# A graph layer whose lists are loaded in two parts, with its edges and pieces of x in another order

## The reference

```python
msg = node_feat[src] + edge_feat                       # 53125 x 128
neigh = segment_sum(msg, dst, num_segments=3125)
rst = (1.0 + eps[0]) * node_feat + neigh
h = rst @ W1 + b1                                      # 256 columns
h = (h - mean(h, 0)) * rsqrt(var(h, 0) + 1e-5) * gamma + beta
out = relu(h) @ W2 + b2
x = layernorm(x + out, axis=-1)
```

## Time and profile before

| | us |
|---|---|
| median of three runs (256.85 to 257.66) | 257.31 |
| the profiled execution, its own time | 256.49 |
| its span, first to last instruction | 254.6 |
| PE busy | 238.1 |
| DVE busy | 184.7 |
| POOL busy | 172.5 |
| ACT busy | 130.1 |

### The profile page before, as it was taken

The page is one execution under the profiler, slowest core; times in us unless marked ns, Lnnn a source line. Parts: engine busy times, 40 slices in busy tenths (PEclk is TensorE's granted clock), DMA queues, the critical chain, the costliest instruction groups (busy, mean ns, idle before and its releaser), DMA issues.

```text
span 254.6 us, 6682 instructions
## 1 busy us (share of the span) xinstructions
PE 238.1 (94%) x2080; PEld 197.2 (77%) x2080; DVE 184.7 (73%) x706; ACT 130.1 (51%) x229; POOL 172.5 (68%) x114
## 2 busy tenths in 40 slices
PE   7579999899999999999999999999999999999980
PEld 3569678788889988888878888888888888644970
DVE  2899888998989888887878777865757311388872
ACT  2343366665556655655544544544443320386794
POOL 4667557888888888888888888888888870550000
PEclk9755699999999999999999999999999999999998
DMA  4799878988988988887878887878676320000033
GB/s 114 237 243 238 223 175 196 260 218 180 213 190 184 209 183 209 192 193 189 198 168 178 190 190 165 188 164 179 155 162 130 63 36 8 0 0 5 0 126 130
DMA packets 38189, 40.00 MB, mean 157 GB/s; under 512 B 5330, under 2 KB 25864, under 8 KB 38152
## 3 DMA queue, kind: packets, MB, share of 16 engines
q1 hardware_dynamic: 23176, 32.70, 44.3%
q0 software_dynamic: 14400, 6.56, 21.5%
q10 hardware_dynamic: 576, 0.28, 0.5%
HBM read 37.92 MB, written 1.60 MB: 155 GB/s over the span
## 4 chain that ended last, share of the span: by engine, by line
PE 66%; DVE 8%; POOL 7%; DMA 7%; issue 5%; ACT 3%; DVEq 1%; SPq 1%; ACTq 0%; POOLq 0%
PE ps L736 21%; PE ps L745 17%; PE ps L772 9%; POOL egat L538 7%; PE ps L766 6%; PE ps L715 4%; PE ps L844 4%; DMA ebuf<-in_edge_lists_dram 3%; DVE hit_k L1043 2%; PE ps L830 2%; PE ps L763 2%; DMA egat<-in_x_dram,srci 2%; DVE aggT L1125 2%; DMA aggT<-in_x_columns_dram 2%; PE ps L696 2%
## 5 line engine op out<-in xcount | busy, mean ns | idle before, releaser
L538 POOL DMA_INDIRECT egat<-in_x_dram,srci x100 | 162.9, 1629 | 42.6 <-issue 27.1
L624 ACT ACTIVATE big<-ps 128x500 f32 x158 | 96.4, 610 | 91.0 <-PE ps L772 89.8
L745 PEld LDWEIGHTS ps<-hit_c,ebuf 128*128 128x128 f32 x632 | 104.5, 197 | 13.9 <-DVE aggT L1125 4.5
L745 PE MATMUL ps<-hit_c,ebuf 128*128 128x12 f32 (+1 forms) x632 | 96.9, 228 | 5.3 <-DMA ebuf<-in_edge_lists_dram 2.7
L1125 DVE TENSOR_TENSOR aggT<-aggT,ps 128x20 f32 x208 | 36.1, 173 | 47.3 <-PE ps L745 35.3
L736 PE MATMUL ps<-big,xN 128*128 128x120 f16 (+7 forms) x200 | 58.2, 293 | 0.3 <-ACT big L624 0.3
L736 PE MATMUL ps<-big,xr 128*128 128x120 f16 (+7 forms) x200 | 58.3, 293 | 0.0
L736 PE MATMUL ps<-big,x_room 128*128 128x120 f16 (+7 forms) x200 | 58.2, 293 | 0.0
L772 PE MATMUL ps<-hit_k,hit_l 128*128 128x375 f16 x158 | 55.3, 350 | 0.0
L766 PE MATMUL ps<-hit_k,hit_l 128*128 128x300 f16 x158 | 47.0, 297 | 0.0
L1043 DVE TENSOR_TENSOR hit_k<-iota_b,key 128x752 f16<-128x752 f16 x79 | 43.1, 546 | 0.2
(11 more groups left out here) (95 smaller groups left out, 182.3 us busy)
## 6 DMA issues: line engine op xcount, KB each, us to landing
ebuf<-in_edge_lists_dram SPq DMA_DIRECT2D x79, 256.0 KB, 3.4
egat<-in_edge_lists_dram SPq DMA_DIRECT2D x50, 128.0 KB, 3.1
egat<-in_x_dram,srci POOLq DMA_INDIRECT x100
aggT<-in_x_columns_dram SPq DMA_DIRECT2D x6, 256.0 KB, 3.9
xN<-in_x_rows_dram SPq DMA_DIRECT2D x6, 256.0 KB, 3.5
out_dram<-big SPq DMA_DIRECT2D x5, 256.0 KB
w_sb<-in_L_gnn_W_dram SPq DMA_DIRECT2D x2, 128.0 KB
out_dram<-big SPq DMA_DIRECT2D x2, 128.0 KB
```

The lines of the kernel that those rows point to most:

```text
L538: return nc.gpsimd.indirect_dma_start(to, None, x[:, :], bass.IndirectOffsetOnAxis(ap=ix, axis=0), compute_op=op)
L624: nc.scalar.activation(cnt[:, :, bass.ds(lows[m - load_from(m)], WIN)], ps[:, m % BANKS_C, 0:KEYS].rearrange("p (t n) -> p t n", n=WIN), A ...
L745: last = nc.tensor.matmul(ps[:, SUMS + w % BANKS_S, c0:c0 + n], rows_v[:, j * D:(j + 1) * D], hits_v[:, 0:n], start=(j == 0), stop=(j == R ...
```

## The change

- The lists of the first 17 groups (`FIRST`) are loaded first, by DMAs of their own; the rest of the lists follows later in the head. DVE waits for the rest at window 2 (`W_LISTS`), where it also makes the places of the gathered groups.
- Chunk 0 is asked for ahead of slot 0. Piece 0 of x by rows is loaded at window 1 instead of in the head; the other pieces follow.
- Pieces 0, 2, 4 and 5 of x are split on TensorE (before: 3, 4 and 5), pieces 1, 3 and 6 on DVE (before: 0, 1, 2 and 6). Their windows change with them.
- Blocks 0, 4 and 5 hold 12, 30 and 30 groups in place of 10, 31 and 31. The planner's costs change; the gathered groups then stand at windows 7, 11, 15, 18, 23 and so on, where they stood at 4, 8, 12, 16, 21.
- 11 matmuls in the head in place of 17. b2 is loaded by SyncE at window 40, not by ACT's queue in the head.

```diff
-BLOCKS_C = (10, 12, 17, 25, 31, 31, 22, 10)
+BLOCKS_C = (12, 12, 17, 25, 30, 30, 22, 10)
-SPLITS_W = (5, 8, 12, 20)
-RESTS_W = (14, 17, 20)
-ROWS_W = (1, 4, 7, 9, 12, 15)
-COLUMNS_W = (1, 20, 23, 26, 29, 32)
-SCALES_W = (5, 27, 31, 35, 39, 43)
+SUMMED = (0, 2, 4, 5)
+SPLITS_W = (10, 16, 26)
+RESTS_W = (7, 13, 19, 23)
+ROWS_W = (1, 4, 7, 10, 13, 16, 19)
+COLUMNS_W = (1, 22, 25, 28, 31, 34)
+SCALES_W = (5, 30, 33, 36, 39, 43)
-STAGES_W = (4, 14, 18)
-W_IDENT = 4
+STAGES_W = (5, 14, 20)
+W_LISTS = 2
+W_IDENT = 5
-HITS = 2400
-HITS_W = 12
+HITS = 2280
+HITS_W = 16
-GATHER_FIRST = 9000
+GATHER_FIRST = 15000
-FILL_HEAD = 17
+FILL_HEAD = 11
...
-        SUM_B = [early_g - 1, early_g, early_g + 1]
+        SUM_B = list(SUMMED)
...
+        FIRST = STAGES[0] + 1
...
-            sp.dma_start(dst_l, dst).then_inc(dst_loaded, 16)
-            sp.dma_start(starts_l, starts.unsqueeze(0).to_broadcast([P, G])).then_inc(dst_loaded, 16)
+            starts_p = starts.unsqueeze(0).to_broadcast([P, G])
+            sp.dma_start(dst_l[:, 0:FIRST * ROWS], dst[:, 0:FIRST * ROWS]).then_inc(first_lists_loaded, 16)
+            sp.dma_start(starts_l[:, 0:FIRST], starts_p[:, 0:FIRST]).then_inc(first_lists_loaded, 16)
...
+            chunk(0)
             slot(0)
             sp.dma_start(firsts[:, :], starts.unsqueeze(0)).then_inc(firsts_loaded, 16)
-            chunk(0)
             columns_piece(T_ORDER[0])
+            sp.dma_start(dst_l[:, FIRST * ROWS:T], dst[:, FIRST * ROWS:T]).then_inc(lists_loaded, 16)
+            sp.dma_start(starts_l[:, FIRST:G], starts_p[:, FIRST:G]).then_inc(lists_loaded, 16)
             chunk(1)
             slot(1)
-            rows_piece(0)
             for w in range(G):
                 if w in X_AT:
                     sp.wait_ge(window_summed, w + 1)
-                    rows_piece(1 + X_AT.index(w))
+                    rows_piece(X_AT.index(w))
...
+                    sp.dma_start(b2_l[:, :], b2.unsqueeze(0).to_broadcast([P, D])).then_inc(b2_loaded, 16)
...
-            act.dma_start(src_l, src[:, 0:GC * ROWS]).then_inc(src_loaded, 16)
+            act.dma_start(src_l[:, 0:FIRST * ROWS], src[:, 0:FIRST * ROWS]).then_inc(first_lists_loaded, 16)
...
-            act.dma_start(b2_l[:, :], b2.unsqueeze(0).to_broadcast([P, D])).then_inc(b2_loaded, 16)
+            act.dma_start(src_l[:, FIRST * ROWS:], src[:, FIRST * ROWS:GC * ROWS]).then_inc(lists_loaded, 16)
...
-            dve.wait_ge(dst_loaded, 32)
-            dve.wait_ge(src_loaded, 16)
+            dve.wait_ge(first_lists_loaded, 48)
             stage_places(0)
...
-                if w == 0:
+                if w == W_LISTS:
+                    dve.wait_ge(lists_loaded, 48)
                     nearness(GC, G, rel_gathered_made)
-                if w == 1:
+                if w == W_LISTS + 1:
                     dve.wait_ge(rel_gathered_made, 1)
                     hits_g(0)
```

More of the change, by code:

```diff
@@ L277, in gnn_layer @@
         ps = ctx.enter_context(nc.psum_tensor("ps", [P, 8, BANK], F32))
-        dst_loaded = sem("dst_loaded")
-        src_loaded = sem("src_loaded")
+        first_lists_loaded = sem("first_lists_loaded")
+        lists_loaded = sem("lists_loaded")
         firsts_loaded = sem("firsts_loaded")
@@ L401, in store_of @@
             return next(m for m in range(GC) if C_AT[m] >= w)
-        assert len(SPLIT_AT) == len(SPLIT_B) and len(REST_AT) == len(SUM_B) and len(X_AT) == len(T_AT) == len(SCALE_AT) == NB - 1
+        assert len(SPLIT_AT) == len(SPLIT_B) and len(REST_AT) == len(SUM_B) and len(T_AT) == len(SCALE_AT) == len(X_AT) - 1 == NB - 1
         STAGES = list(STAGES_G) + [GC]
@@ L425, in gnn_layer @@
         W_LAST = W_TESTS - 2
+        FIRST = STAGES[0] + 1
+        assert W_LISTS + 1 < G_AT[0] and W_LISTS < STAGES_W[0]
         TEST_F = next(f for f in range(1, F) if READY[f] + 5 > W_TESTS + 8 * TEST_STEP)
```

## The result

The changed kernel takes 259.16 us (median of five runs, 258.49 to 263.42) against 256.85 (256.48 to 257.66) for the kernel before beside it: 1.0076 of its time, 95% interval [1.0054, 1.0098]. It is slower by 0.8%, where 254.0 us and "faster" were forecast. A later repeat, of eleven runs, gave 1.0080 [1.0056, 1.0104].

The account below looks back on a forecast made before the run. TensorE and GpSimd were both taken to reach the end nearly without slack. DVE's 2.9 us and the 0.53 us final wait summed to 3.4, 3.3 kept: from the 257.31 us median to 254.0, range 252.2 to 256.6.

Parts of the forecast that it names:

- the start: Head: lists land at 3.7 us, 1.5 us earlier for DVE; TensorE's first edges near 6.2, 3.3 us earlier.
- Block 0 of 12 groups: Loop: products start at window 15, not 13; nothing is added, some 0.3 us moves behind window 18.
- the pause at window 4: Early loop: a 1.1 us pause for the gather, which covered DVE catching up, goes as gathered groups come later.
- Four pieces split on TensorE: Pieces of x: DVE loses 1.36 us of subtractions; TensorE gains 1.4 us of work, or 2.7 at 1.2 GHz.
- it rises by 26 us rather than 30.2: Early loop: the piece at window 13 brings back TensorE's clock, leaving TensorE 2.9 us ahead.
- if the piece at window 7 does so: Early loop: that piece brings back the clock, TensorE leads DVE from 16 us on; DVE's 2.9 us hold.
- 2.9 us earlier at any window past 20 or so: Loop, by DVE: 1.5 us from earlier lists plus 1.4 from fewer subtractions; 1.9 more at window 18.
- a sign that the gathers set the end: End: a last gather no earlier than 207 us would mean GpSimd's supply, not the head, set the end.
- A: Rival, window 2: waits for remaining lists and chunk 1 replace the first wait; gain 1.6, time 255.7 us; chance 0.16.
- B: Rival, early loop: clock stays at 1.2 GHz through window 19; 1.0 us later, time 258.3 us; chance 0.09.
- C: Rival: clock never falls or rises at once, TensorE never held; gain 5.0, time 252.3 us; chance 0.13.
- D: Rival, end: GpSimd's ring sets the pace; gain 2.2 to 2.8, time 254.8 us; inside the forecast's 0.60.

Follow-up runs that it names:

- The head alone: Kernel before with only lists in two parts, chunk 0 third, b2 at window 40 and 11 head matmuls: 0.9937 of its time, 255.91 us.
- the control: Changed kernel with the same eight register loads moved earlier, to windows that still have key comparisons: 1.0079 of the kernel before.
- the blocks alone: Kernel before with only the block sizes changed, to 12, 12, 17, 25, 30, 30, 22, 10: 0.9954 of its time.

## Why the prediction was wrong

**Right: the start.** DVE's first list operation at 4.35 us (3.3 to 4.6 forecast) and the first edges on TensorE at 6.80 (5.7 to 6.5, so 0.3 late). Chunk 0 took about 5.1 us from its issue at 1.70, where 3.4 to 4.0 were forecast; as the keys were made by 6.76, little hung on it. The lists took 3.1 us from their issue at 1.22. By the Trainium skill, "DMA: Bandwidth & Descriptors", on the anatomy of one DMA, they would have been there at 3.3; the page fitted its rule to DMAs that GpSimd issues, and these are SyncE's. The trace is 1.05 us above it, so a term by that rule would have been worse. The head alone gained 1.6 us, against 3.3 for TensorE's start and 1.5 on DVE: the smaller term is what reached the end. That DVE sets it is argued, not shown.

**Failed, and decisive: "*Block 0 of 12 groups*", "nothing is added".** The new order of gathered groups at 7, 11, 15 was costed at nothing, and the pause at window 4 even as cover. The columns do add up to the same; what differs is on DVE. Its register loads, 1.1 us each, were in no term, since they count as busy nowhere. The old order put one of them on key comparisons between windows 8 and 120, the new one six, and the new blocks put tests right ahead of two. Moving eight loads gave back 0.76% (1.0080 to 1.0004), about 2.0 us, the control none of it. Three of them gave back 1.4 us. That the place of the loads costs this is shown; how much of it is the comparisons behind a load, and how much the empty queue ahead of it, is not.

**Failed: "*Four pieces split on TensorE*".** The gain of 1.36 us on DVE was carried to the end, and TensorE's 1.4 to 2.7 left to its slack. Alone this part costs 0.37%, 1.0 us, with an interval from 0 to 1.9. By the table it is a mean over two cases: where the piece at window 7 brings back the clock the part gains 1.2 us (256.2 against 257.4), else it loses 1.7 (259.1). Two of the changed kernel's pieces run at 1.2 GHz (18.23 and 26.92 us, 2.05 for the float32 part).

**Failed: "it rises by 26 us rather than 30.2".** In the changed kernel it rises in 29 to 30 us. The clock by microsecond:

```profile
28.00:29.00 1.00, 1.00 (x3) 0.22 (x2) 0.97 (x6) 0.00 (x0) 0.00 (x0) 0.50 0.68 231
29.00:30.00 1.00, 1.00 (x9) 0.80 (x8) 0.49 (x3) 0.56 (x1) 0.73 (x1) 0.71 0.01 2
```

The second of the named cases, "if the piece at window 7 does so", did occur, with the old order. By the table above it is worth 1.5 to 2.9 us.

**Failed: the sums.** "2.9 us earlier at any window past 20 or so" measured 0.17 at window 20, and slot 6 was asked for at 34.51 us, forecast 31.3. So 2.7 of the 5.2 us between forecast and result are missing at window 20 already, ahead of the loads at 22 and after. The term took DVE for the engine that sets the pace. But from 9.5 to 36.1 us DVE is busy for 20.88 us now and TensorE, at 1.2 GHz for most of it, for 24.03. The head alone loses its lead there too, with the old order and pieces: its two profiles are 1.63 and 1.29 us ahead at window 8, and 0.45 behind and 0.56 ahead at window 18. GpSimd:

```profile
207.98 1.54 POOL L545 DMA_INDIRECT egat<-in_x_dram,srci  x1 [0.30 <-issue]
```

The last gather, at 207.98 us, did come no earlier than 207, which the forecast named as a sign that the gathers set the end. They didn't: TensorE takes these rows at 213.73 and waits for nothing there, where it stopped 0.53 us in the earlier trace rows. Both were late because the windows were.

**The rivals.** A: chunk 1 was 2.03 us late as it said, the lists were not; it costs at most a part (0.4%) and isn't shown to turn the sign. B had the sign and nearly the size (258.3), and half of its mechanism: the clock stayed low, but until 29.7 and not past 34, and window 18 was summed 1.87 us earlier where B had 0.9 at best. The loss lies behind it. The rule of the Trainium skill, "TensorE: Matmul & The Clock Gate", part 1, that activity releases the throttle, fits the piece at 18.23 that brought no rise behind a stop, and the one at 26.92 that did. C, the clock that never falls, did not occur: all profiles show the longer durations from a time between 7.6 and 11.8 us on. D is refuted, the wait for the last gather is gone.

**The account.** From the forecast to the result there are 5.2 us. 2.0 are the place of the loads (shown); 1.5 to 2.9 the late clock (an estimate from runs of four kernels, sorted by it); the rest is in the head (1.6 us in place of 3.3) and the pieces. These last three are not independent, as the head's lead and the pieces both pass through the stretch at 1.2 GHz. Open are: why a stop in front of the piece goes with a late clock; why the blocks alone gain 0.46%; how much of the order's cost on the kernel before is the loads, which weren't moved there; what moving only the two tests would give, which no run did; and the falls at 62 to 64 us, seen in two profiles. Head, pieces and plan sum to +0.27% and make +0.76% together, for which the early clock lost with the new order is the likely reason, not a shown one.

## What to carry to other kernels

Cost what the page doesn't call busy: an engine that loads registers makes nothing new until the load is done, and "issue", or a releaser that was long done, is where it hides. Beside work that the engine has queued the load is nearly free (0.1 to 0.5 us idle here), behind an empty queue it costs all of its 1.1 us and more. When an order of work changes, lay it over every periodic event of each engine, and not over the sums alone, which stay equal. Lay it over tests and other rare steps too, which move with the blocks. And test parts by themselves: of this change the head alone is 0.6% faster than the kernel before.

## What the runs showed of the hardware

- A register load of 16 int32 numbers by DVE takes 1.1 us when it begins at a multiple of 16 numbers, and 3.7 us when it runs across one (medians of eleven loads, most of them such; 3.67 and 3.65 us in two kernels).
- A register load runs while DVE finishes what it has queued: 76.07 to 77.16 us beside comparisons until 76.90, with 0.20 us idle. With nothing queued, from 78.04 on, the same load leaves it idle for 1.23 us.
- The record of the granted clock can miss a fall: five profiles read 1.00 where a matmul of 375 columns took 494 ns, as at 0.50. The durations are the safer mark.
- By the mean clock of its runs, the same kernel returns to 2.4 GHz early or late from run to run, which makes an estimated 1.5 to 2.9 us. In two profiles the clock fell again in mid-loop, behind stops of 0.7 to 1.0 us, at a price of about 8 us, an estimate; the changed kernel had a stop of 0.83 us there and the one with the blocks alone stops of 0.83 and 0.73, and neither fell.
